# Stage one of a two-layer block: rope in front of the head blocks, mantissa work at the end of a step

## The reference

```
xn  = layernorm(x)
# layer 0, attention
q, k, v = split(xn @ Wqkv.T + bqkv)
q, k    = rope(rmsnorm(q, gq)), rope(rmsnorm(k, gk))        # rotate pairs by cos and sin
qf, kf  = relu(q), relu(k);  vpad = [v, 1]
vk      = einsum('bhlp,bhld->bhpd', vpad, kf)
res     = einsum('bhpd,bhld->bhlp', vk, qf)
attn    = res[..., :-1] / (res[..., -1:] + 1e-6)            # the quotient
out     = rmsnorm(attn @ Wout.T + bout, gout)
# layer 0, feed-forward: both operands rounded to a 6-bit grid in blocks of 32
scale   = max(max|block| / 7.5, 1e-30);  xd = nearest_on_grid(xn / scale) * scale
ffn     = xd @ wd.T + bias                                  # wd: the weight, rounded likewise
x = x + out + ffn
# layer 1 (stage two of the kernel, apart from its projections)
xn2 = layernorm(x);  x = x + attention(xn2) + routed_experts(xn2)
```

## Time and profile before

| | |
|---|---|
| runs | 365.11 us median of 3 (364.57 to 365.88) |
| profiled execution | 366.06 us, of which the span is 364.2 us |
| busy share of the span | DVE 85%, PE 84%, POOL 66%, ACT 51% |
| chain that ended last | DVE 37%, PE 25%, issue 15%, POOL 12%, ACT 7% |
| granted TensorE clock, mean | 0.975 |

### The profile page before, as it was taken

One profiled execution on the slowest core, in us unless ns is written; L12 is line 12 of the kernel. 1 busy time (PEld: TensorE's weight loads), 2 busy tenths in 40 slices (PEclk: granted clock), 3 DMA queues, 4 the chain that ended last, 5 costly groups with the idle time before them and its releaser, 6 DMA issues.

```text
span 364.2 us, 4906 instructions
## 1 busy us (share of the span) xinstructions
PE 307.7 (84%) x1371; PEld 218.2 (60%) x1371; DVE 311.2 (85%) x825; ACT 186.4 (51%) x507; POOL 239.0 (66%) x152
## 2 busy tenths in 40 slices
PE   0569876989899887685988999999989999998993
PEld 0336664768677776563655755656657566565662
DVE  5995899987977868947989899898998989989792
ACT  3345756878678578491342632536236361352611
POOL 3185587655736531107779868889888998889651
PEclk9987999999999999699899999999999999999999
DMA  4690000000000000019633324225343252335000
GB/s 138 175 276 1 2 0 1 3 1 0 3 0 3 0 0 3 0 33 169 161 92 80 114 62 121 81 67 137 116 100 99 76 137 73 101 106 132 3 29 29
DMA packets 21311, 24.81 MB, mean 68 GB/s; under 512 B 2428, under 2 KB 12068, under 8 KB 21284
## 3 DMA queue, kind: packets, MB, share of 16 engines
q1 hardware_dynamic: 20336, 24.09, 25.0%
q10 hardware_dynamic: 820, 0.39, 0.4%
q0 software_dynamic: 128, 0.01, 0.0%
HBM read 22.13 MB, written 2.36 MB: 67 GB/s over the span
## 4 chain that ended last, share of the span: by engine, by line
DVE 37%; PE 25%; issue 15%; POOL 12%; ACT 7%; DMA 3%; SPq 1%; ACTq 0%; DVEq 0%; POOLq 0%
PE Q L917 11%; POOL prod_qk L856 8%; PE VN L917 7%; PE T L917 3%; DVE att L1549 3%; DVE rope_b L1326 3%; DVE rope_a L1324 3%; DVE hid L1587 3%; DVE sgc L1574 3%; POOL prod_pv L866 2%; PE T L913 2%; DVE bst L1167 2%; DVE attn L1356 2%; ACT L750 1%; DMA cw<-comb_table 1%
## 5 line engine op out<-in xcount | busy, mean ns | idle before, releaser
L856 POOL TENSOR_TENSOR prod_qk<-qkv 128x1024 f32<-128x1024 f32 x32 | 76.3, 2395 | 17.0 <-DVE above L1419 15.2
L866 POOL TENSOR_TENSOR prod_pv<-prob,qkv 128x1024 f32<-128x1024 f32 x32 | 69.6, 2195 | 18.5 <-DVE att L1549 17.0
L917 PE MATMUL VN<-hid,w 128*128 128x512 f32 x144 | 74.6, 599 | 1.5 <-DVE hid L1587 1.5
L917 PE MATMUL Q<-xT_hi,w_hi 128*128 128x512 f32 x72 | 52.1, 724 | 0.2 <-ACT sg L750 0.2
L1587 DVE TENSOR_TENSOR hid<-T,sgc 128x512 f32<-128x512 f32 x64 | 43.4, 679 | 0.0
L1535 DVE TENSOR_REDUCE scr<-prod_qk 128x128 f32<-128x1024 f32 x32 | 38.8, 1213 | 5.0 <-POOL prod_qk L856 4.9
L917 PE MATMUL Q<-bias,ones 128*128 128x400 f32 (+1 forms) x64 | 30.3, 474 | 15.1 <-ACT v_ext L638 7.1
L917 PE MATMUL T<-xT_hi,w_hi 128*128 128x512 f32 x72 | 30.8, 428 | 9.4 <-DVE hid L1587 9.3
L1549 DVE TENSOR_REDUCE att<-prod_pv 128x128 f32<-128x1024 f32 x32 | 38.3, 1197 | 0.0
L750 ACT ACTIVATE VN<-Q 128x512 f32<-128x512 f32 x32 | 18.6, 582 | 36.7 <-PE Q L917 29.1
L750 ACT ACTIVATE ND<-Q 128x512 f32<-128x512 f32 x32 | 18.6, 582 | 35.7 <-PE Q L917 24.7
(11 more groups left out here) (176 smaller groups left out, 747.9 us busy)
## 6 DMA issues: line engine op xcount, KB each, us to landing
cw<-comb_table SPq DMA_DIRECT2D x64, 256.0 KB, 4.5
out_x<-fin SPq DMA_DIRECT2D x8, 256.0 KB, 4.5
x<-in_x SPq DMA_DIRECT2D x2, 256.0 KB, 3.0
wraw<-in_w1T SPq DMA_DIRECT2D x1, 512.0 KB, 4.1
w3raw<-in_w3T SPq DMA_DIRECT2D x1, 512.0 KB, 4.7
w<-in_w2T SPq DMA_DIRECT2D x1, 512.0 KB, 5.7
rope_s<-in_c_sin ACTq DMA_DIRECT2D x1, 256.0 KB, 4.9
rope_c<-in_c_cos SPq DMA_DIRECT2D x1, 256.0 KB, 5.4
```

The costliest lines, as they stand in the source:

```text
L856: pool.tensor_tensor(prod_qk[:, t % 2], bc(qkv2[:, TH * half + t, j, 0:D], 1, NB), qkv2[:, :, j, D:2 * D], ALU.mult).then_inc(qk_prod, 1)
L866: pool.tensor_tensor(prod_pv[:, t % 2].rearrange("p (h e) b -> p b h e", e=HD), bc(prob[:, t].rearrange("p h b -> p b h"), 3, HD), qkv2[:, ...
L917: return pe.matmul(o, lhsT, rhs, start=start, stop=stop)
```

## The change

It reorders parts of `step` on four engines, and adds one wait.

- DVE: `rope_tile(0)` stands in front of `head_blocks` and `plus_ffn`; `mx_magic` stands behind `xn2T_lo_part`, in front of the statistics, where it was behind `rope_tile(1)` and in front of `attention`; `weights_l0` stands in step 0, in front of `rope_table`, where it was in step 1. `mx_scales` waits for the `xd` of the chunk before, since POOL now multiplies by those scales later.
- POOL: the two instructions of `rope_add` are parts of their own and stand in front of `mx_round`; `weight_rounded` stands in front of all steps.
- PE and ACT: the projection `l1_tile(2)` and its copy stand in front of `xd_transposes` and `xdT_evac`.

The diff:

```diff
@@ ACT, step
                 if i > 1:
                     run(i, 1, xnT_evac)
+                run_next(i, 5, l1_tile(2))
                 run(i, 2, xdT_evac)
                 weights_of_step(i)
-                run_next(i, 5, l1_tile(2))
@@ POOL
-            def rope_add(c):
-                after(pool, feat_ready, c)
-                after(pool, qfT_ps, c)
-                for h in range(2):
+            def rope_add(h):
+                def part(c):
+                    if h == 0:
+                        after(pool, feat_ready, c)
+                        after(pool, qfT_ps, c)
                     js = slice(2 * h, 2 * h + 2)
                     pool.wait_ge(qkv_rope, NJ * c + 2 * h + 2)
                     pool.tensor_tensor(rope_ab[:, js].rearrange("p j n f -> p j (n f)"), rope_a[:, js, :],
                                        rope_b[:, js, :], ALU.add).then_inc(rope_sum, 1)
+                return part
...
+            weight_rounded()
...
                 run(i, 3, residual)
+                run(i, 1, rope_add(0))
+                run(i, 1, rope_add(1))
                 run(i, 1, mx_round)
-                if i == 1:
-                    weight_rounded()
-                run(i, 1, rope_add)
@@ DVE, mx_scales
                 dve.wait_ge(mx_scale, 3 * c + 1)
+                after(dve, xd_ready, c)
@@ DVE, step
                 if i == 0:
+                    weights_l0()
                     rope_table(1)
...
+                run(i, 1, rope_tile(0))
                 run(i, 2, head_blocks)
                 run(i, 3, plus_ffn)
...
-                run(i, 1, rope_tile(0))
                 run(i, 1, rope_tile(1))
-                run(i, 1, mx_magic)
-                if i == 1:
-                    weights_l0()
                 run(i, 2, attention)
                 run(i, 1, rope_tile(2))
                 run(i, 1, rope_tile(3))
                 run(i, 4, xn2T_lo_part)
+                run(i, 1, mx_magic)
                 run(i, -1, stats(0, stats1_ready))
```

## The result

The changed kernel takes 370.29 us (median of 6 runs, 367.93 to 370.78), the kernel before, beside it, 365.72 us (364.57 to 366.06): a ratio of 1.0119, 95% interval 1.0097 to 1.0141. By the ratio it is slower by 4.4 us (the medians are 4.6 apart). Its profiled execution took 370.23 us, with a span of 368.4.

What follows compares the result with a forecast made beforehand. DVE and PE bound stage one, each waiting for the other once per step; POOL's rounding joins the cycle. 1.3 + 1.1 + 1.2 + 0.4 − 0.6 = +3.4 us: 369.5 profiled, 368.5 median; own range 366.0 to 371.0, overall 364.4 to 372.6.

Steps and rivals of the forecast that it cites:

- start and step 2: Program start and step 2: weight preparation delays PE's first product 1.3 us, late xd adds 1.1; together +2.4.
- steps 3 and 4: DVE-bound steps, where held instructions and rope 0 lengthen the way to vk_bd: +1.2 and +0.4 us.
- steps 5 to 8: Full steps of stage one: 14.92 us each, 0.15 less than before, −0.6 us over four steps.
- step 9: Gains 1.30 us again and loses about as much to xd; taken as nothing, between −0.5 and +0.6.
- stage two: Part after stage one: starts later by the sum, with no term of its own.
- V to T: From V (DVE begins vk_bd) to T (xT_lo done; steps 1 to 3: last rope done): 5.08 us, gain 1.30.
- L1313 held behind the rope sum: DVE's first mxm instruction, at T, waits for POOL's second rope sum, ends T + 1.03; xd ready T + 5.34.
- L1187 slips in between two POOL instructions: Small DVE instruction queued behind L1181 runs right after it, ahead of POOL's third rounding instruction.
- first rival: L1187 waits for POOL's third rounding instruction, 1.05 us more: +4.6 us, 373.1; chance 0.16.
- T to V: From T to the next V: 9.84 us instead of 8.70, as PE waits for POOL's rounding.
- second rival: L1313 not held, xd by T + 4.8, step 14.27: −3.2 us, 361.9; chance 0.13.
- swap on PE and ACT: Projection in front of xd's transposes: included in the figures; without it PE would hold the projection up behind xd.

Runs made afterwards that it cites:

- second pair: Kernel before and changed kernel each profiled once more, unchanged: 364.23 us and 370.63 us, one run each.
- Experiment 3: Changed kernel with POOL's second rope sum moved behind its rounding: 365.97 us, ratio to the kernel before 0.9997.
- experiment 4: Changed kernel with the projection l1_tile(2) and its copy behind the transposes of xd again: 376.0 us, ratio to the kernel before 1.0305.
- 6: Changed kernel with the second rope sum behind the rounding and the weight's preparation in a gap of step 1: 364.53 us, ratio to the kernel before 0.9971.
- experiment 7: Changed kernel, rope sum behind rounding, weight in step 1's gap; steps 1 to 3 in old order (mantissa pair before quotient, rounding before rope sums): 362.56 us, ratio 0.9918.
- experiments 2: Kernel before with only tile 0's rope moved in front of the head blocks: 366.93 us, ratio to the kernel before 1.0024.
- experiment 8: Kernel before with tile 0's rope ahead of the head blocks and, except in step 1, the mantissa pair behind the quotient: 367.92 us, ratio 1.0075.

## Why the prediction was right, and which terms were mis-sized

Slower was right, and of the reasons given the late start, the longer steps 2 to 4 and POOL's rounding on the path all show. The point, 368.5, was 1.8 us low; 0.6 of this is the kernel before, which took 365.72 beside the changed one and not 365.11. In the first pair of profiles the terms are 1.60 (start and step 2), 1.49 (steps 3 and 4), 0.18 (steps 5 to 8), 0.44 (step 9) and 0.53 (stage two), 4.2 us together, where 2.4, 1.6, −0.6, 0 and 0 were forecast. In the second pair they are 3.27, 1.08, 0.22, 1.71 and 0.10, 6.4 together. That the total fell inside the range is in part luck: in the first pair the first two terms had been taken too high and the last three too low, and the sizes of the start, step 9 and stage two change from one execution to the next. The bounds given for the terms add up to 365.3 to 371.2; the range that was stated, 366.0 to 371.0, is narrower than they are. Step by step:

- **V to T, 5.08:** 5.06. The rope and the mantissa pair left this half, and the numerators were late next.
- **L1313 held behind the rope sum, about 1.03 long, `xd` at T + 5.34:** 1.08 and T + 5.38. Experiment 3 shows that the order of the two POOL parts is the cause. The Trainium skill ("SBUF — State Buffer", section "Who interferes with whom") states an exclusive lock between GpSimd and such DVE instructions; 1.08 us beside the sum and 0.42 without it agree with that. The 0.5 us more that its order of issue would put on the start do not show: PE's first product came 1.23 later, my value without them being 1.3.
- **L1187 slips in between two POOL instructions:** as L1190 it took 0.16 at 103.73, and POOL's third began at 103.87. The first rival fell.
- **T to V, 9.84:** mis-sized, 10.05. The transposes of `rope_ab` came at T + 6.87, not T + 6.68: those of `xd` took 0.66 instead of 0.60, and 0.15 instead of 0.05 passed behind ACT's copy. So a step takes 15.11 and not 14.92, and the term of steps 5 to 8, −0.6, is +0.2. It was the difference of two large numbers (−1.30 and +1.14), and 0.2 turned its sign: a gain was forecast where there is none.
- **Steps 3 and 4, +1.2 and +0.4:** V of step 2 to V of step 3 is +0.94 (+0.96 in the second pair of profiles); step 4 +0.55, and +0.12 in the second pair. In the first profile of the changed kernel PE's granted clock was 0.51 from 60 to 62 us, in the second 1.00. In step 2 V to T is 4.42 (4.41 was worked out), and T to V 1.63 longer than before instead of 1.9. Rope 0 stands in front of V of step 3 without idle time, and L1320 (1.38) is the held one, as said; in step 4 of the first profile DVE was idle for 0.35 between them.
- **Start and step 2, +1.3 and +1.1:** PE's first product at 13.65 (13.7 was named), the transposes of `xd` 28.80 (28.95), the product behind them 29.57 (29.75). But V of step 2 came at 34.43, not 35.2: PE's granted clock returned to 2.4 GHz earlier in the step, and the last product took 0.92 where it had taken 1.48. That is a matter of the single execution: the second pair of profiles gives 34.68 − 31.41 = 3.27, the first 1.60. The 2.4 lies between; one pair can't tell it better.
- **Step 9, taken as 0:** mis-sized, +0.44 in the first pair, +1.7 in the second (15.56 against 13.85 from V of step 8 to V of step 9). PE has nothing left between the transposes of `xd` and those of `rope_ab` (the projection went in front, and no chunk is left for a q, k, v product there), so both waits (0.62 and 0.78) show, and in the second execution the clock fell behind them.
- **Stage two:** shifted along, as said. Its ninth `hid` comes 53.8 to 55.7 behind V of step 9 in all twelve profiles; the changed kernel's two (54.6, 53.9) lie on both sides of the first of the kernel before (54.1).
- **The second rival** named the condition under which it turns: `xd` by about T + 4.8 and no hold. Experiment 3 made both true (T + 4.72, 0.42) and got 14.46 a step; 14.27 had been worked out. Its total of 361.9 was not reached (365.97): it put +0.9 on the start and steps 2 to 4, where V of step 4 is 2.88 later than before.
- **The swap on PE and ACT:** said to be needed, and experiment 4 shows it: 0.6 us a step, as expected, in two of the four steps from V of step 4 to V of step 8, and 2.2 in the other two, where the clock fell.

Open: what decides in an execution where the clock stands at its lower level in step 2, in step 9 and behind PE's wait in stage two, and why stage two is longer in experiments 3, 6 and 7, the three with the sum behind the rounding (55.0 to 55.7 from V of step 9 to the ninth `hid`, against 53.8 to 54.9 in the others).

## What to carry to other kernels

Before a part is moved on one engine, write down which POOL instruction will be running when each DVE instruction that only touches SBUF comes up. Not each of them is held: L1302, a reduction of 512 values per partition, took 0.67 us beside POOL's third rounding instruction in the changed kernel (103.81), and as L1299 0.68 with POOL idle in the kernel before (101.28); POOL's took 1.05 in either. But moving a part that can be held moves the hold, and in three of these kernels (the changed one and experiments 2 and 8) the hold took back what the move had won in a full step. A slack (here 2.7 us on `xd`) is spent once: a part moved behind the last handover of a step uses it whole, and everything that is then in front of it on the other engine counts. The same order needn't be best for all steps: the fastest kernel here (experiment 7) has the old order in steps 1 to 3 and the new one from step 4 on.

## What the runs showed that was not expected

Two executions of one program differ by 1.4 us at V of step 2 (32.83 and 31.41), with the granted clock at 0.50 or at 1.00 at the same place; so the start of a kernel is not to be read from one pair of profiles. An instruction on 12 values per partition, 0.17 long where nothing holds it, took 0.97 beside POOL (experiment 8). In experiment 4 PE waited 1.98 to 1.99 us for `xd` in four steps running; behind two of these waits the transposes took 0.66, behind the other two 0.97 and 1.11, at the lower clock.
